# A GRU kernel on one core: the reset gate joint at place 7 too, and VectorE's work around it in another order

## The reference

```python
def step(h, inp):
    x_t, prop = inp
    comb = jnp.concatenate([x_t, h], axis=-1)
    z = jax.nn.sigmoid(comb @ Wz + bz)
    r = jax.nn.sigmoid(comb @ Wr + br)
    comb2 = jnp.concatenate([x_t, r * h], axis=-1)
    h_cand = jnp.tanh(comb2 @ Wh + bh)
    h_new = (1.0 - z) * h + z * h_cand
    h_next = jnp.where(prop, jnp.tanh(h_new @ Wp + bp), h_new)
    return (h_next, h_new)
_, ys = jax.lax.scan(step, h0, (xs, do_prop))
return x + jnp.transpose(ys, (1, 0, 2))        # x: (64, 128, 512) float32
```

## Time and profile before

| | |
|---|---|
| median of 3 runs | 1040.63 us (1039.86 to 1040.64) |
| the profiled execution, its own time | 1040.76 us |
| its span in the trace | 1038.9 us |
| TensorE (PE) busy | 1033.4 us, 99% |
| VectorE (DVE) busy | 880.9 us, 85% |
| ScalarE (ACT) busy | 777.0 us, 75% |
| granted TensorE clock | 1.00 over the span |

### The profile page before, as it was taken

One profiled execution on the slowest core, in us unless ns is written; L12 is line 12 of the kernel. 1 busy time (PEld: TensorE's weight loads), 2 busy tenths in 40 slices (PEclk: granted clock), 3 DMA queues, 4 the chain that ended last, 5 costly groups with the idle time before them and its releaser, 6 DMA issues.

```text
span 1038.9 us, 48087 instructions
## 1 busy us (share of the span) xinstructions
PE 1033.4 (99%) x20746; PEld 953.2 (92%) x20746; DVE 880.9 (85%) x2880; ACT 777.0 (75%) x1789; POOL 0.2 (0%) x4
## 2 busy tenths in 40 slices
PE   9999999999999999999999999999999999999998
PEld 4577999999999999999999999999999999999998
DVE  6978888898989899898989989989898998876666
ACT  6877777777878778777887777878777777665565
POOL 0000000000000000000000000000000000000000
PEclk9999999999999999999999999999999999999999
DMA  9312211001111011110011110111100100000001
GB/s 331 110 43 84 84 54 44 23 23 43 43 43 43 4 44 42 44 43 23 23 44 43 44 43 11 35 44 43 44 29 17 43 23 23 23 10 17 24 24 44
DMA packets 38484, 47.26 MB, mean 45 GB/s; under 512 B 2176, under 2 KB 34048, under 8 KB 37888
## 3 DMA queue, kind: packets, MB, share of 16 engines
q1 hardware_dynamic: 38000, 44.12, 12.6%
q10 hardware_dynamic: 272, 0.07, 0.0%
HBM read 27.40 MB, written 16.78 MB: 43 GB/s over the span
## 4 chain that ended last, share of the span: by engine, by line
PE 98%; DMA 1%; SPq 0%; DVE 0%; issue 0%; ACT 0%; DVEq 0%
PE acc L1360 38%; PE x_acc L1274 34%; PE acc L1368 17%; PE x_acc L1164 8%; DMA x_part<-wz_dram 1%; PE x_acc L1295 0%; SPq L419 0%; SPq L416 0%; DVE mag_win L982 0%; SPq L425 0%; SPq L424 0%; DVE x_lo L889 0%; PE acc L1170 0%; ACT gate L745 0%; DVE new L1099 0%
## 5 line engine op out<-in xcount | busy, mean ns | idle before, releaser
L1274 PE MATMUL x_acc<-x_hi,win_hi 128*128 128x256 f16 x1092 | 298.0, 273 | 0.0
L1274 PE MATMUL x_acc<-x_lo,win_hi 128*128 128x256 f16 x1092 | 297.9, 273 | 0.0
L1274 PE MATMUL x_acc<-x_hi,win_lo 128*128 128x256 f16 x1092 | 297.9, 273 | 0.0
L589 ACT ACTIVATE gate<-gate,unscale 128x128 f32<-128x128 f32 (+1 forms) x316 | 128.6, 432 | 136.4 <-DVE gate L1067 77.7
L595 ACT ACTIVATE gate<-acc,unscale 128x128 f32<-128x128 f32 (+1 forms) x384 | 123.8, 371 | 97.9 <-PE acc L1360 97.7
L1368 PE MATMUL acc<-h_split,wrec_hi 128*128 128x128 f16 x2704 | 178.8, 220 | 0.0
L1360 PE MATMUL acc<-h_split,wrec_lo 128*128 128x64 f16 x4096 | 177.5, 194 | 0.0
L1360 PE MATMUL acc<-q_split,wrec_hi 128*128 128x64 f16 x4000 | 162.2, 194 | 0.0
L555 ACT ACTIVATE x_part<-x_acc,bias,part_unscale 128x256 f32<-128x256 f32 x312 | 154.6, 561 | 6.4 <-PE x_acc L1274 5.5
L1360 PEld LDWEIGHTS acc<-h_split,wrec_lo 128*128 128x128 f16 x4096 | 154.2, 98 | 4.7
L1368 PEld LDWEIGHTS acc<-h_split,wrec_hi 128*128 128x128 f16 x2704 | 153.7, 98 | 0.0
(11 more groups left out here) (141 smaller groups left out, 1517.5 us busy)
## 6 DMA issues: line engine op xcount, KB each, us to landing
out_dram<-x_blk SPq DMA_DIRECT2D x30, 512.0 KB, 3.2
x_blk<-x_dram SPq DMA_DIRECT2D x24, 512.0 KB, 3.8
x_blk<-x_dram SPq DMA_DIRECT2D x3, 1024.0 KB, 8.7
x_part<-wz_dram SPq DMA_DIRECT2D x4, 256.0 KB, 6.8
x_part<-wh_dram SPq DMA_DIRECT2D x4, 256.0 KB, 6.6
x_part<-wr_dram SPq DMA_DIRECT2D x1, 1024.0 KB, 10.9
x_part<-wz_dram SPq DMA_DIRECT2D x1, 1024.0 KB, 13.1
x_part<-wh_dram SPq DMA_DIRECT2D x1, 1024.0 KB, 15.3
```

Source lines behind the costliest of these rows:

```text
L589: nc.scalar.activation(gate[g][:, half], gate[g][:, half], func, scale=unscale[:, g:g + 1]).then_inc(gate_ready[g], 1)
L1274: mm = nc.tensor.matmul(in_halves(x_acc[bank][:])[:, j], weights[g][:, slot_w, k, j * P:(j + 1) * P], in_halves(values[m % 2][:, slot_x, : ...
```

## The change

Four things change, all within steps 14 to 111.

1. The reset gate is joint at place 7 too, so in steps 23, 31, ... 103 (11 steps). TensorE does 32 matmuls in place of 48 for it and 4 matmuls of stage 18 ahead of the candidate; VectorE gets two reduces; ScalarE's seed is the double one.
2. Where the next step has a joint reset gate and this one doesn't propagate (steps 18 to 107, places 0, 1, 2, 4, 5 and 6, 68 steps), each low part is made right behind the full state of its own half.
3. `end_quarter` of stage 17 goes from the end of place 6 to behind the propagation at place 7; at place 7 `end_quarter` of stage 19 goes ahead of `add_states` of that step.
4. In steps 22, 30, ... 102 the states of places 4, 5 and 6 are added to the output at the end of place 6, no more behind the propagation at place 7.

```diff
-JOINT_RESET_AT = (0, 1, 2, 3, 4, 5, 6)
-JOINT = range(19, 109)
+JOINT_RESET = range(19, 109)
+JOINT = JOINT_RESET
+ENDS_AT = [(), (4,), (5,), (), (11, 12), (), (), (19,)]
+END_BEHIND_PROPAGATION = 17
+STATES_AHEAD_AT = 6
...
         def joint_reset(t):
 
-            return joint(t) and t % BLOCK in JOINT_RESET_AT
+            return t in JOINT_RESET
...
+        def states_ahead(t):
+
+            return joint(t) and t % BLOCK == STATES_AHEAD_AT
+
+        def low_by_half(t):
+
+            return joint_reset(t + 1) and not propagates(t)
...
                     nc.vector.tensor_tensor(h_out[:, half, :], new[:, half, :], keep[:, half, :], ALU.subtract).then_inc(h_new_ready, 1)
+                    if low_by_half(t):
+                        dve.wait_ge(hi, count + n + 1)
+                        dve.wait_ge(h_new_ready, 2 * t + n + 1)
+                        subtract_hi(h_out, split, half).then_inc(lo, 1)
                 for n, half in enumerate(HALVES):
-                    dve.wait_ge(hi, count + n + 1)
-                    dve.wait_ge(h_new_ready, 2 * t + n + 1)
-                    subtract_hi(h_out, split, half).then_inc(lo, 1)
+                    if not low_by_half(t):
+                        dve.wait_ge(hi, count + n + 1)
+                        dve.wait_ge(h_new_ready, 2 * t + n + 1)
+                        subtract_hi(h_out, split, half).then_inc(lo, 1)
+                ends = ENDS_AT[s] if m + 1 in SEVEN else ()
+                if prop:
+                    for n in ends:
+                        end_quarter(m + 1, n)
+                if states_ahead(t):
+                    dve.wait_ge(h_new_ready, 2 * t + 2)
+                    add_states(t + 2 - CHUNK, t + 1)
...
-                for n in stages_of(t)[0] + stages_of(t)[1]:
-                    if ORDER[n][1] in (5, 6):
+                if not prop:
+                    for n in ends:
                         end_quarter(m + 1, n)
...
-                    add_states(t + 1 - CHUNK, t)
+                    if not states_ahead(t - 1):
+                        add_states(t + 1 - CHUNK, t)
+                    if s == BLOCK - 1 and m + 1 in SEVEN:
+                        end_quarter(m + 1, END_BEHIND_PROPAGATION)
```

More of the change, by code:

```diff
@@ L374, in behind_propagation @@
         def behind_propagation(t):
-            return propagates(t) and joint(t) and joint(t + 1)
+            return propagates(t) and t + 1 in JOINT_RESET
         def joint_reset(t):
-            return joint(t) and t % BLOCK in JOINT_RESET_AT
+            return t in JOINT_RESET
         def joint_candidate(t):
-            return joint(t) and t % BLOCK in JOINT_CANDIDATE_AT
+            return t in JOINT_RESET and t % BLOCK in JOINT_CANDIDATE_AT
+        def states_ahead(t):
+            return joint(t) and t % BLOCK == STATES_AHEAD_AT
+        def low_by_half(t):
+            return joint_reset(t + 1) and not propagates(t)
         def resets_before(t):
```

## The result

The changed kernel is slower by a little: 1042.13 us in the median of 17 runs (1040.99 to 1043.04), the kernel before 1040.19 us in 17 runs (1039.5 to 1041.61); ratio 1.0016, 95% interval 1.001 to 1.0022. I had forecast 1040.2 us in a range up to 1041.6, and "within 0.2%". The change is within 0.2%, but the time lies outside the range and the sign is the other one.

What follows compares the result with a forecast made beforehand. TensorE bounds the kernel, matmul behind matmul. Terms: -0.44 (columns) -0.44 (steps 47 and 95) +0.44 (stage 20's new wait) = -0.44 us, from 1040.76 to 1040.3, as a median 1040.2 us; range 1039.2 to 1041.6.

Steps and rivals of the forecast that it cites:

- a release: TensorE starts 0.06 us behind the end of what it waits for; any margin above that is free.
- Part 1: Joint reset gate at place 7: TensorE gains 0.04 us a step, 0.44 us over 11 steps.
- Part 2: End of place 7: stage 20 newly waits 0.04 to 0.05 us for `end_quarter` of stage 19, 0.44 us in all.
- Steps 47 and 95: Place 7: these two steps fall from 9.71 to 9.49 us, a gain of 0.44 us; bounds 0 to 0.44.
- part 4: Low parts by half, 68 steps: dependent pairs cost 0.32 us, not 0.20; second low part 0.24 us later, covered, so nothing.
- +1.0 us for four such hesitations: Low parts by half: upper bound if VectorE's 0.25 us hesitations reach TensorE on thinner margins; value taken was zero.
- Rival B: Hesitations land on thinner margins, four to six times 0.25 us; time near 1041.4 us; chance 0.2.
- Rival C: Dependent low part costs more than taken, making q late; about 5 us slower at w = 0.2, 1045; chance 0.02.
- w: Price of a wait on a neighbour's result on VectorE, in place of 0.035 us; all shifts by 2 x (0.085 + w).
- the low part's own margin: Second low part before TensorE takes it, step 67: 0.42 us, of which 0.24 goes and 0.06 is needed; nothing lost.
- Part 3: Swap of `end_quarter` 17 and the three states: the additional 0.66 us falls into 0.61 us idle time; nothing.

Runs made afterwards that it cites:

- experiment 6: The changed kernel with 50 small memsets added at VectorE's start, moving its later instructions 50 places on; 1042.08 us against 1040.62 for the kernel before, ratio 1.0014.
- experiment 1: The changed kernel without the low parts by half, all else as changed; 1040.59 us against 1040.48 for the kernel before, ratio 1.0001.
- experiment 3: The changed kernel with the two waits of a low part by half in the other order; 1040.67 us against 1040.48 for the kernel before, ratio 1.0002.
- experiment 5: The kernel before with only the reset gate at place 7 made joint, VectorE's other order kept; 1049.28 us against 1040.62, ratio 1.0081.

## Why the prediction was wrong

**What held.** TensorE bounds the kernel, and a release takes 0.06 us. Part 1: 0.029 and 0.056 us a matmul, and place 7 takes 9.50 us where I said 9.49. The 81 ns that the Trainium skill gives in "TensorE: Matmul & The Clock Gate", section Back-to-back issue gap, for a matmul of 128 columns in a stream of weight loads and matmuls show in no joint step: it is 56 ns in all. Part 2: stage 20 waits in every block. In step 63 of the changed kernel `end_quarter` starts 549.63 - 542.25 = 7.38 us into the step, to the hundredth what I took from step 67, and stage 20 starts 0.05 us behind its end:

```profile
549.23 0.49 DVE L1043 TENSOR_TENSOR q_split<-h_ring,q_split 128x128 f16<-128x128 f32 x2
549.63 0.75 DVE L980 SCALAR_TENSOR_TENSOR x_part<-x_acc,part_unscale,x_part 128x512 f32<-128x512 f32 x1
```

```profile
550.43 0.28 PE L1300 MATMUL x_acc<-x_hi,win_hi 128*128 128x256 f16 x1
```

Steps 47 and 95 are at 9.50 us, as forecast, though luck has a share in it: the changed kernel has no stop in them, and in experiment 6, where one falls into another step of place 7, step 71 takes 9.68 us. With the low parts left alone (experiment 1) these parts sum to 713.20 - 713.40 = -0.2 us in the trace, where I had -0.44; the difference is step 64 with its 0.24.

**The step that failed** is in part 4: "So each dependent pair costs 0.285 + 0.035 = 0.32 in place of 0.20". I took the price of a dependence from instructions with one wait. A low part has two, and the late one stands ahead of it. It cost 0.39 to 0.40. The shift of the second low part was 0.39 us in place of 0.24, and against the margin that I had myself worked out, 0.42 with 0.06 needed, the difference decides: 0.42 - 0.24 leaves 0.18, 0.42 - 0.39 leaves 0.03. A release needs 0.06, so TensorE waits 0.03 us at places 3 and 6 in every block, 0.8 us in all with the 0.006 of place 1. Where the row gives 0.24 (experiment 3), the term is zero as forecast.

**The second term that was mis-sized** is what hesitations cost. I had "+1.0 us for four such hesitations" as a bound beside a value of zero: in the profiled execution the longer steps sum to 1.3 us, and 0.6 before. The points at which VectorE can stop are the same 21 in both (experiment 6). With thinner margins more of them reach TensorE, though not all. Steps 22, 73 and 86 (0.12, 0.35 and 0.12 us) are longer because the second low part is late; for 22 and 86 a stop of 0.11 us was enough, too short for the table of experiment 6. In steps 26 and 90 (0.09 each) the reset gate's reduce is late, and q with it. Step 64 (0.24) follows a stop ahead of a low part of q, as in experiment 1; step 65 behind it (0.10) is longer only with the low parts by half. The stops listed for steps 30, 59, 81 and 94 cost nothing. Rival B named the mechanism and put it at 1041.4. The toll, 0.9 us in all places, which it lacked, would make it 1042.3, against 1042.1 measured.

**Rival C** had the right mechanism, a dependent low part that costs more than I took, and the wrong place. By its sum the idle time at place 1 is used up from w = 0.07, and q is late from there on. It was w = 0.10, the idle time is used up indeed, and q moves by 0.005 us. The sum had left out that the reduce, which doesn't need its neighbour's result, can overlap with it: it starts at 433.72, 0.06 us ahead of the end of the instruction before it (433.56 + 0.22 in the trace). What broke first was the low part's own margin, which I had dismissed in one sentence.

**The price of a neighbour's result.** The Trainium skill, "VectorE: DVE Perf Modes", section The DRAIN you can't avoid, reports of eight copies in a row that they take the same time with a semaphore after each as with one after the last. The runs agree as long as the value is there already: the low parts of the kernel before have a wait of their own and follow each other at 0.20 us. Where the wait is for the instruction directly ahead, the start-to-start distance is 0.12 us longer with the wait in the instruction (0.32 against 0.20) and 0.19 longer with the wait ahead of it, for operations of 0.285 us. How much of the 0.12 is the semaphore and how much the need for the result, no run separates.

**Part 3** came out at nothing, as said, but I hadn't seen what it was worth: experiment 5 shows 0.4 us a block lost without it.

## What to carry to other kernels

Before a producer and its consumer are put side by side on one engine, price the dependence for exactly that instruction, with all its waits: what it loses is the overlap with an independent neighbour, and the order in which two waits are written can add more than half to that (here 0.19 in place of 0.12 us). In a kernel whose bound engine never stops, list the margin of each value that it takes, and subtract every shift from each of them; a "nothing" that leaves 0.03 us where a release needs 0.06 is a loss in every block, and more as soon as anything hesitates. A matmul form that saves instructions and not columns saved next to nothing here: two matmuls of 64 columns take 0.058 us, one of 128 takes 0.056.

## What the runs showed of the hardware that I had not expected

- Which of two waits stands ahead of the instruction changes a dependent pair on VectorE from 0.32 to 0.39 us start to start, and with it the whole kernel from 1042.1 to 1040.7 us, with no other difference in the program.
- VectorE stops for some 0.25 us (0.46 together with a late wait) at points that lie 128 instructions of its own stream apart, counted with its semaphore instructions, whatever stands there, and a packet of 8192 bytes of queue 14, whose kind is "instruction", starts 0.6 to 0.9 us behind the late instruction.
